# Sums and low halves of B's blocks: from VectorE instructions to adding transfers issued by GpSimd

## The reference

```
h   = grouped_conv1d(x, weight, 4 groups, 9 taps) + (cond @ c_weight.T)[:, :, None] + bias[None, :, None]
q   = h @ Wq.T                      # 16 numbers for each row of 1024
s   = q @ keys.T                    # 64 scores
top = top 16 of s;  w = softmax(top);  gate = w at the 16 experts, 0 elsewhere
z   = (h @ A.T) * gate              # 512 numbers, 8 for each expert
out = x + 2 * (z @ B.T)             # 512 -> 1024
```

## Time and profile before

| | |
|---|---|
| median of 3 runs | 233.98 us |
| the profiled execution, its own time | 234.5 us |
| its span (first to last instruction) | 232.7 us |
| instructions | 4036 |
| PE / DVE / ACT / POOL busy | 97% / 84% / 54% / 3% |
| granted TensorE clock | 1.0 in all 40 slices |
| moved by DMA | 40.89 MB, 176 GB/s |

### The profile page before, as it was taken

How to read it: one execution, slowest core, us unless ns; L and a number is a source line. 1 busy time by engine, 2 the same in 40 slices (tenths; PEclk the granted TensorE clock), 3 DMA queues, 4 the chain that set the end, 5 groups by cost and what they waited for, 6 DMA issues and landing times.

```text
span 232.7 us, 4036 instructions
## 1 busy us (share of the span) xinstructions
PE 224.6 (97%) x1351; PEld 198.4 (85%) x1351; DVE 194.7 (84%) x443; ACT 126.3 (54%) x317; POOL 7.6 (3%) x16
## 2 busy tenths in 40 slices
PE   8999999999999999799989899999999999999995
PEld 6789998898988889688878889898898889898884
DVE  1799889999799797998999899989999896877442
ACT  4897758266491653727645584927484655252100
POOL 2010062000000000000000000000000000000000
PEclk9999999999999999999999999999999999999999
DMA  6997047749855425637360425854374156347552
GB/s 195 360 394 306 1 142 266 263 137 317 262 200 142 149 99 158 205 114 220 119 207 13 129 86 143 265 136 139 97 234 150 34 176 198 111 143 267 159 201 93
DMA packets 24869, 40.89 MB, mean 176 GB/s; under 512 B 2832, under 2 KB 11920, under 8 KB 24848
## 3 DMA queue, kind: packets, MB, share of 16 engines
q1 hardware_dynamic: 24704, 40.55, 53.6%
q10 hardware_dynamic: 144, 0.08, 0.2%
HBM read 28.04 MB, written 12.58 MB: 175 GB/s over the span
## 4 chain that ended last, share of the span: by engine, by line
DVE 58%; PE 22%; issue 14%; ACT 4%; DVEq 0%; POOL 0%; ACTq 0%; POOLq 0%
DVE x_lo L1095 9%; DVE h_t L1137 7%; DVE h_lo L1095 7%; DVE x_blk L1119 5%; PE p_z L888 5%; DVE a_raw L1266 3%; DVE zt_lo L1095 3%; DVE x_nat L1284 2%; DVE a_raw L1198 2%; DVE a_lo L1095 2%; DVE sc_b L1249 2%; DVE x_nat L1298 2%; DVE bt_lo L1095 2%; DVE e_top L1254 1%; PE p_out L937 1%
## 5 line engine op out<-in xcount | busy, mean ns | idle before, releaser
L509 ACT ACTIVATE h_hi<-h_t 128x1024 fp32r<-128x1024 f32 x16 | 17.1, 1066 | 40.0 <-DVE h_t L1137 40.0
L888 PEld LDWEIGHTS p_z<-a_hi,h_hi 128*128 128x128 f32 x240 | 32.6, 188 | 2.5 <-issue 0.3
L888 PE MATMUL p_z<-a_hi,h_hi 128*128 128x264 f32 x240 | 34.3, 285 | 0.0
L888 PE MATMUL p_z<-a_hi,h_lo 128*128 128x264 f32 x240 | 34.1, 285 | 0.0
L888 PE MATMUL p_z<-a_lo,h_hi 128*128 128x264 f32 x240 | 34.0, 284 | 0.0
L888 PEld LDWEIGHTS p_z<-a_hi,h_lo 128*128 128x128 f32 x240 | 31.2, 188 | 0.0
L888 PEld LDWEIGHTS p_z<-a_lo,h_hi 128*128 128x128 f32 x240 | 31.1, 188 | 0.0
L1095 DVE TENSOR_TENSOR x_lo<-x_blk,x_hi 128x1536 fp32r<-128x1536 f32 (+4 forms) x18 | 25.3, 1406 | 2.3 <-ACT x_hi L509 2.3
L929 PE MATMUL p_out<-b_hi,zt_hi 128*128 128x512 f32 (+1 forms) x64 | 25.0, 393 | 0.0
L930 PE MATMUL p_out<-b_hi,zt_lo 128*128 128x512 f32 (+1 forms) x64 | 24.7, 388 | 0.0
L559 ACT ACTIVATE p_conv<-p_conv,u 128x128 f32<-128x128 f32 x88 | 23.6, 356 | 1.7 <-PE p_conv L837 1.4
(11 more groups left out here) (160 smaller groups left out, 400.6 us busy)
## 6 DMA issues: line engine op xcount, KB each, us to landing
x_nat<-in_x_rows SPq DMA_DIRECT2D x16, 512.0 KB, 4.0
out_dram<-x_nat SPq DMA_DIRECT2D x31, 256.0 KB, 3.1
x_blk<-in_x_blocks SPq DMA_DIRECT2D x14, 516.0 KB, 3.6
z_dram<-a_raw SPq DMA_DIRECT2D x64, 64.0 KB, 1.8
a_raw<-z_dram SPq DMA_DIRECT2D x16, 256.0 KB, 2.9
a_raw<-in_a_wq SPq DMA_DIRECT2D x8, 264.0 KB, 7.0
x_nat<-in_b_w SPq DMA_DIRECT2D x4, 512.0 KB, 9.6
a_raw<-in_b_w SPq DMA_DIRECT2D x3, 512.0 KB, 4.2
```

The source lines that it names most:

```text
L509: nc.scalar.activation(dst, src, ACT.Copy).then_inc(s, 1)
L888: mm = nc.tensor.matmul(z_bank(t, b)[:, 0:HB], h[:, t % 2, r, :], a[:, r, b * HB:(b + 1) * HB], start=k == 0 and r == 0, stop=k == 2 and r ...
```

## The change

- SP loads only B11 (into `b_left`) and B12 (into `b_right`), once the low halves of A are written, now ahead of z_out(2) and z_in(2).
- Each sum is formed by a transfer that GpSimd issues and that adds a block from DRAM to `b_left` or `b_right` in SBUF (`accum_op=ALU.add`).
- ACT writes the high half as before and, by a second ACTIVATE with scale -1, the negated high half into `bt_lo`. A second adding transfer, SBUF to SBUF, adds the sum to that: sum - high.
- ACT's split_bt is moved in its pass to ahead of split_w, sum_w and split_h.
- DVE's `sum_b` and `split_bt` are gone. PE waits for the low halves by one semaphore each.
- GpSimd has the eight adding transfers in a written order, with waits where one needs another.

```
-        b_sums = (a_raw[:, 3:5, 0:J], a_raw[:, 5:7, 0:J], h_c[:, 0].rearrange(...))
+        b_left, b_right = a_raw[:, 3:5, 0:J], a_raw[:, 5:7, 0:J]
+        b_sums = (b_left, b_left, b_right, b_left)
 (sync)
-            def load_b(k, rows, half):
-                sp.dma_start(b_sums[(0, 1, 2, 1)[k]], b_w[:, 2 * rows:2 * rows + 2, half * J:(half + 1) * J]).then_inc(s_bt[k], 16)
+            def load_b(k, dst, half):
+                sp.dma_start(dst, b_w[:, 0:2, half * J:(half + 1) * J]).then_inc(s_bt[k], 16)
...
             load_rows(3)
+            sp.wait_ge(s_alo, R)
+            load_b(0, b_left, 0)
+            load_b(1, b_right, 1)
             z_out(2)
             z_in(2)
-            sp.wait_ge(s_alo, R)
-            load_b(0, 0, 0)
-            load_b(1, 0, 1)
             sp.wait_ge(s_tr, 2 * TW)
-            load_b(2, 1, 1)
...
-                if i == TB + 3:
-                    sp.wait_ge(s_btlo, 3)
-                    load_b(3, 1, 0)
 (gpsimd)
+            def sum_b(k, rows, half):
+                pool.dma_start(b_sums[k], b_w[:, 2 * rows:2 * rows + 2, half * J:(half + 1) * J], accum_op=ALU.add).then_inc(s_btsum[k], 16)
+
+            def split_bt(k):
+                pool.wait_ge(s_btneg, k + 1)
+                pool.dma_start(bt_lo[:, k], b_sums[k], accum_op=ALU.add).then_inc(s_btlo[k], 16)
+
+            pool.wait_ge(s_bt[0], 16)
+            sum_b(0, 0, 1)
+            pool.wait_ge(s_bt[1], 16)
+            sum_b(2, 1, 1)
+            split_bt(0)
+            pool.wait_ge(s_btlo[0], 16)
+            sum_b(1, 1, 1)
+            split_bt(1)
+            pool.wait_ge(s_btlo[1], 16)
+            sum_b(3, 1, 0)
+            split_bt(2)
+            split_bt(3)
 (scalar)
             def split_bt(k):
-                act.wait_ge(s_btsum, k + 1)
-                high(bt_hi[:, k], b_sums[(0, 0, 1, 0)[k]], s_bthi)
+                act.wait_ge(s_btsum[k], 16)
+                high(bt_hi[:, k], b_sums[k], s_bthi)
+                nc.scalar.activation(bt_lo[:, k], b_sums[k], ACT.Copy, scale=-1.0).then_inc(s_btneg, 1)
...
+                if TB <= i < TB + 4:
+                    split_bt(i - TB)
                 if i in (5, 7):
                     split_w(i // 2)
                     sum_w(i // 2)
                 if i + 2 < NT:
                     split_h(i + 2)
-                if TB <= i < TB + 4:
-                    split_bt(i - TB)
 (tensor)
-                    pe.wait_ge(s_btlo, k + 1)
+                    pe.wait_ge(s_btlo[k], 16)
 (vector)
-            def sum_b(k): ...                  # and its calls in passes 3 to 6
-            def split_bt(k): ...               # and its calls in passes 4, 5 (two) and 7
```

More of the change, by code:

```diff
@@ L131, in adaln_ffn @@
         z_g = a_raw[:, 7, 0:J]
-        b_sums = (a_raw[:, 3:5, 0:J], a_raw[:, 5:7, 0:J], h_c[:, 0].rearrange("p (a n) k -> p a (n k)", a=2))
+        b_left, b_right = a_raw[:, 3:5, 0:J], a_raw[:, 5:7, 0:J]
+        b_sums = (b_left, b_left, b_right, b_left)
         z_sums = h_c[:, 0].rearrange("p (s tb) x -> p s tb x", s=2)
@@ L153, in adaln_ffn @@
         s_xn = [sem(f"s_xn{k}") for k in range(XN)]
-        s_bt = [sem(f"s_bt{k}") for k in range(4)]
-        s_btsum = sem("s_btsum")
+        s_bt = [sem(f"s_bt{k}") for k in range(2)]
+        s_btsum = [sem(f"s_btsum{k}") for k in range(4)]
         s_bthi = sem("s_bthi")
-        s_btlo = sem("s_btlo")
+        s_btneg = sem("s_btneg")
+        s_btlo = [sem(f"s_btlo{k}") for k in range(4)]
         s_zsum = sem("s_zsum")
@@ L1192, in sum_z4 @@
                                                in1=z_sums[:, 1, :, 64:P], op0=ALU.mult, op1=ALU.subtract).then_inc(s_zsum, 1)
[L1194 to L1202, removed]
             def split_keys():
@@ L1430, in _ @@
                     split_z1(0)
[L1431 to L1434, removed]
                 if FP + 3 <= i < NT - 1 and i % 2:
@@ L1465, in _ @@
                     split_z12((i - FP - 2) // 2)
-                if i == TB + 2:
-                    split_bt(2)
                 if FP + 3 <= i < NT - 1 and i % 2:
```

## The result

The changed kernel is slower: 241.96 us (median of 4 runs, 240.5 to 242.49) against 234.0 for the kernel before; the ratio is 1.0325, 95% interval 1.0276 to 1.0375. The forecast was 230.9, 1.3% faster. The profiled execution took 241.59 us with a span of 239.8; before it was 234.5 and 232.7.

A forecast was written before the change was run, and what follows sets the result against it. PE was taken to bound the kernel, so only its waits for DVE's work could go: 2.88 + 0.30 + 0.40 = 3.6 us, less 0.5 for collisions, 3.1; 233.98 - 3.1 = 230.9 us. Range 230.1 to 231.6, chance 0.55.

The forecast's parts named there:

- What DVE's work is worth: In passes 3 to 7 DVE loses 9.7 us of work, which saves PE 3.6 us of waits.
- What of it stays: PE's waits for DVE's h_t at conv_sum(10) and conv_sum(11), 0.82 and 0.59 us, mostly stay; 0.4 us in all goes.
- ACT's four copies are hidden: ACT's high and negated copy, 2.12 us a pair, fit in its 3.4 to 4.1 us wait before h_hi.
- 58.5 + 2L: Second sum lands two transfers after ACT's negated copy ends at 58.5 us: at 69.5, L being one transfer's landing time.
- the third sum is issued early: neither matters: The third sum, like the fourth, costs nothing while one adding transfer lands in under 14 us.
- The threshold: In pass 4 PE loses time only if ACT's pair of copies starts later than 73.5 us.
- The L of 5.5: Issue to landing of one 512 KB adding transfer: 2.9 us fixed plus the 1.3 us payload time doubled, 5.5 us.
- The slower rival: ACT waits in pass 4 for the second sum, query chain behind; from 9.3 us per transfer; 234.5 to 245; chance 0.23.
- The deduction of 0.4 to 0.5 us for other transfers: Added transfer load makes z's return and some block loads late, costing PE 0.4 to 0.5 us.
- The first sum: B11 lands at 47 to 48.5 us, its sum at about 54, before ACT reaches it at 56.4.
- The signs of being wrong: Pass 4's bt_hi starts after 73 us, an adding transfer takes over 7.5, or DVE waits for x_blk or z's return.
- DVE held up by GpSimd's issuing: GpSimd's work for eight transfers delays DVE at most 0.5 us each, 4 in all; costed at 0 to 0.5.

The follow-up runs named there:

- no_transfers: Changed kernel with GpSimd's eight transfers cut out, loaded blocks standing in for the sums, low halves only negated high ones: 230.12 us, ratio 0.9837.
- pool_order: Changed kernel with the third sum moved behind the second in GpSimd's order: 230.77 us, ratio 0.9865.
- order0213: Changed kernel with ACT's four pairs in order 0, 2, 1, 3 in passes 3, 4, 5, 7, GpSimd's order fitted: 230.59 us, ratio 0.9885.
- sums_only: Changed kernel with only the four sums by adding transfers, the low halves by DVE as before: 231.0 us, ratio 0.988.

## Why the prediction was wrong

- **What DVE's work is worth: right.** 3.6 us forecast before the deduction for collisions, 4.0 measured without transfers. The five scores waits went in the changed kernel except the one that the transfers made.
- **What of it stays: right.** The h_t waits at conv_sum(10) and (11) are 0.69 and 0.30 us in no_transfers, where 0.82 and 0.59 stood; each was to lose 0.2.
- **ACT's four copies are hidden: right** (no_transfers), if the sum has landed.
- **"58.5 + 2L": this step failed.** The second sum was put at 69.5 and landed at 82.8, 13.3 us later. The trace divides that into three. 4.8 us are a queue that the step left out: GpSimd could not issue the first low half until the third sum, written ahead of it, had landed (65.99 in place of 61.15); the room for descriptors held one adding transfer, and with 1536 bytes of it the low half went at 60.13. I had listed what waits behind ACT, but not what stands ahead in GpSimd's own order; "the third sum is issued early: neither matters" was wrong. 5.8 us are L: 8.9 and 7.4, and 0.4 from the landing of the one to the issue of the other, in place of twice 5.5. And 2.65 us are a late start: ACT was done at 61.15 and not at 58.5, because z's return held zt_hi by 2.3 us where I had allowed 1. The moved loads alone hold it by 0.9 (no_transfers), as allowed; the rest came with the first sum, beside which z took 5.3 us to return in place of 3.2.
- **The threshold: right within 0.7 us.** PE could have had scores(5) at 79.19 in the changed kernel; less the 5.03 us from ACT's pair to scores(5), it loses from a start at 74.16, where I had 73.5. At 82.80 it lost 8.64.
- **The L of 5.5: too small.** No run shows the doubled payload time that it was made of. Inside SBUF adding cost 2.8 us more than the plain transfer of the same queue (medians), from DRAM 2.0 in the one pair in the same place. Would the long L alone have made the change slower? No run keeps it without the queue: in pool_order the two took 6.6 and 6.9 us. As an estimate, 61.15 + 8.94 + 0.41 + 7.43 = 77.9, 3.8 us past the threshold, about what the lighter DVE gives back; and the queue with twice 5.5 would have put the second sum at 65.99 + 11.0 = 77.0, a loss of 2.8. So by this estimate, which leaves the clock out, neither makes the kernel slower by more than some tenths, and both together do.
- **The slower rival** had the right mechanism and place: ACT in pass 4 at the second sum, with split_h and the query behind it. Its deciding point, L = 9.3, was worked out for a chain of two transfers, and the chain had three. As an estimate from the measured start of the third sum (57.78), with three in a row and 0.7 us between them, the 3.5 us given back are gone when the second sum lands at 77.7, at L = 6.4. A chance of 0.23 was too low for a step whose price no row showed and whose queue I had not written out. The clock, which no term held, added 1.8 us.
- **The deduction of 0.4 to 0.5 us for other transfers: right in size,** as far as four executions tell: order0213, with all eight transfers and no wait of ACT for a sum, is 0.5 us above no_transfers.
- **The first sum: late, and harmless.** B11 was put at 47 to 48.5 and landed at 51.15, its sum at 57.5 and not 54. ACT was waiting for z until 58.62 and met the sum without a wait.
- **The signs of being wrong** all came: bt_hi of pass 4 at 82.80 and not before 73, a transfer of 8.9 us, and 3.3 us in which DVE waited for x_blk.
- **DVE held up by GpSimd's issuing: not seen.** h_lo takes 1217 ns in the mean in the changed kernel and 1215 before, and the one h_lo that ran beside the issuing of a transfer took 1219.

## What to carry to other kernels

When work moves from a busy engine to transfers, write out the issuing engine's queue as one chain, with what stands ahead of each item and how many of them can be under way, before pricing any of it; a transfer that nobody awaits can delay one on which everything waits. Put the consumer's wait well behind the landing when there is time to spare: here PE first used a sum at 141.71, 24.9 us after the last low half had landed at 116.86, and taking two sums in another order and two of them a pass later turned 3.3% slower into 1.2% faster (order0213). A faster queue is not always better: with room for two adding transfers at once order0213 became 2.3 us slower, and loads that DVE needed sooner came late.

## What the runs showed of the hardware

- An adding transfer of 512 KB takes 5.2 to 8.9 us from issue to landing in the changed kernel and up to 10.5 in other runs (sums_only), and 1.2 to 1.35 us of GpSimd. A plain one on the same queue takes 3.7 to 4.3 us inside SBUF, 4.1 to 9.3 from DRAM, and 0.7 to 0.9 us of GpSimd.
- With 1024 bytes a partition for descriptors GpSimd issues the next adding transfer only when the last has landed, and where the program has no wait there the trace calls that idle time "issue"; with 1088, 1280 and 1536 it issues two at once. Two plain loads from DRAM of the same size, with 144 packets each in place of 272, go out at once with 1024.
- In the changed kernel PE had no work for 8.5 us; its granted clock was at 0.50 from 81.5 us, within that wait, to 91.7 us, 3.9 us after its end. The work behind the wait took 1.8 us longer than before.
